# One score matmul a head over 48 stacked rows, and two normalisations moved from DVE to POOL

## The reference

```python
q = split_heads(hidden_states_query @ Wq.T + bq)      # query: the layer-normed tokens
k = split_heads(hidden_states_key @ Wk.T + bk)        # key, value: the context
v = split_heads(hidden_states_key @ Wv.T + bv)
scores = einsum('bhqd,bhkd->bhqk', q * 16 ** -0.5, k) + (1 - mask) * -10000.0
ctx = einsum('bhqk,bhkd->bhqd', softmax(scores), v)   # 16 heads
```

## Time and profile before

| | us |
|---|---|
| three runs | 1442.6, 1450.26, 1454.12 (median 1450.26) |
| the profiled execution | 1443.42, with a span of 1441.8 |
| PE busy | 1264.8 (88%) |
| DVE busy | 1092.9 (76%) |
| ACT busy | 1003.9 (70%) |
| POOL busy | 827.7 (57%) |
| first phase | from 0 to about 465, its loop from 26 on |
| mean granted clock of PE | 0.944 of full speed |

### The profile page before, as it was taken

One profiled execution on the slowest core, in us unless ns is written; L12 is line 12 of the kernel. 1 busy time (PEld: TensorE's weight loads), 2 busy tenths in 40 slices (PEclk: granted clock), 3 DMA queues, 4 the chain that ended last, 5 costly groups with the idle time before them and its releaser, 6 DMA issues. The chain is left out here.

```text
span 1441.8 us, 44028 instructions
## 1 busy us (share of the span) xinstructions
PE 1264.8 (88%) x13508; PEld 916.7 (64%) x13508; DVE 1092.9 (76%) x3110; ACT 1003.9 (70%) x2584; POOL 827.7 (57%) x1204
## 2 busy tenths in 40 slices
PE   5999999999985599999998999999999985389994
PEld 3788888888864245656665556656566653278993
DVE  4899999999984268887887877878788873367772
ACT  3988788887883368787776777777787872155662
POOL 3645444454455445777676776777677675045663
PEclk9999999999997699999999999999999996599997
DMA  6233343333400148877666766767576784753323
GB/s 172 86 120 112 106 121 98 118 99 121 120 24 17 48 92 160 159 137 148 136 148 136 151 137 140 141 145 156 122 146 138 146 186 85 285 173 60 61 35 74
DMA packets 303968, 175.19 MB, mean 122 GB/s; under 512 B 250234, under 2 KB 291586, under 8 KB 300720
## 3 DMA queue, kind: packets, MB, share of 16 engines
q1 hardware_dynamic: 287632, 130.94, 40.8%
q0 software_dynamic: 13168, 35.80, 9.8%
q10 hardware_dynamic: 3024, 6.47, 1.6%
HBM read 64.48 MB, written 41.96 MB: 74 GB/s over the span
## 5 line engine op out<-in xcount | busy, mean ns | idle before, releaser
L1663 ACT ACTIVATE b_prob<-b_prob,b_top 112x487 f32<-112x487 f32 x256 | 178.9, 699 | 42.8 <-DVE b_top L1789 40.9
L1296 POOL TENSOR_TENSOR b_halves<-b_prob,b_halves 112x487 f16<-112x487 f32 x128 | 152.3, 1190 | 88.4 <-ACT b_halves L1688 86.6
L1474 PE MATMUL b_ps_p<-w_s,b_tok_s 128*128 128x512 f16 (+1 forms) x768 | 187.7, 381 | 5.6 <-DVE b_k_s L1776 5.3
L1474 PE MATMUL b_ps_p<-b_tok_s,w_s 128*128 128x487 f16 x768 | 188.0, 384 | 4.7 <-POOL b_tok_s L1290 3.7
L1789 DVE CUSTOM_DVE_ANT_0 b_prob<-b_ps_s,b_keep 112x487 f32<-112x487 f32 x256 | 167.7, 656 | 32.1 <-PE b_ps_s L1567 31.8
L701 ACT ACTIVATE a_prob<-a_prob,a_top 112x375 f32<-112x375 f32 x256 | 156.4, 611 | 4.5 <-DVE a_top L837 3.4
L1688 ACT ACTIVATE b_halves<-b_prob 112x487 f16<-112x487 f32 x256 | 156.0, 609 | 0.4
L837 DVE CUSTOM_DVE_ANT_0 a_prob<-a_ps_s,a_keep 112x375 f32<-112x375 f32 x256 | 138.6, 541 | 21.8 <-PE a_ps_s L593 19.2
L1582 PEld LDWEIGHTS b_ps_o<-b_v_s,b_pT 128*128 128x128 f16 (+1 forms) x3072 | 124.9, 100 | 32.7 <-DMA b_pT<-b_halves 11.0
L1582 PE MATMUL b_ps_o<-b_v_s,b_pT 128*128 128x64 f16 (+1 forms) x3072 | 136.1, 195 | 9.0 <-DMA b_pT<-b_halves 8.9
L842 DVE TENSOR_TENSOR a_pT<-a_ps_t,a_pT 125x336 f16<-125x336 f32 x256 | 128.6, 503 | 18.4 <-ACT a_pT L708 12.4
(11 more groups left out here) (262 smaller groups left out, 3063.0 us busy)
## 6 DMA issues: line engine op xcount, KB each, us to landing
xs<-a_blank SPq DMA_DIRECT2D x14, 1032.0 KB, 4.0
c_w_pool<-w_split SPq DMA_DIRECT2D x8, 1600.0 KB, 10.9
b_wch_f<-in_w_experts POOLq DMA_DIRECT2D x32, 384.0 KB, 4.9
w_split<-b_wch_s POOLq DMA_DIRECT2D x32, 384.0 KB, 4.0
a_ctx_f<-in_ctxT SPq DMA_DIRECT2D x16, 375.0 KB, 3.9
a_k_stack<-a_k_s SPq DMA_DIRECT2D x64, 93.8 KB, 2.8
b_ctx_t<-in_ctx SPq DMA_DIRECT2D x16, 375.0 KB
c_xt<-xs SPq DMA_DIRECT2D x35, 129.0 KB, 2.5
```

The source lines that it names most:

```text
L1296: pool.tensor_tensor(halves[:, h % TURN, LO, 0:NK], prob[:, h % RING, 0:NK], halves[:, h % TURN, HI, 0:NK], ALU.subtract).then_inc(s_lo[1], 1)
L1474: last = pe.matmul(out, sta(a, k), mov(m, k), start=(k == 0 and n == 0), stop=(k == tiles - 1 and n == 2))
L1663: act.activation(prob[:, h % RING, 0:NK], prob[:, h % RING, 0:NK], ACT.Exp, bias=top[:, h % RING:h % RING + 1], scale=-1.0, accum_out=sums ...
```

## The change

Each head now gets 48 rows of its own: three parts of 16 rows, for the queries HI, HI, LO and for the keys HI, LO, HI, so that one matmul adds up the three products. Even heads stand in rows 0 to 47, odd heads in rows 64 to 111, in `q_stack` and `k_stack` (8 heads beside each other in the free dimension). A head's scores are one matmul of 48 rows and 375 columns. The queries are no longer doubled: PE makes them with 12 matmuls for 24, ACT moves them out with 2 instructions for 4, and POOL splits 224 columns for 448. To get into the stacked rows, keys and queries go through DRAM: one DMA writes all halves out (`keys_out`, `queries_out`), SP waits until it has landed, and six DMAs of 16 rows each read them back (`stack_keys`, `stack_queries`). SP issues `keys_out` ahead of the tokens of batch b+2, and `stack_queries` behind `clear_rows`. The zeroing of `q_masked` falls away. Wq is loaded with half its columns left out, in two DMAs of 256-byte pieces, and DVE rearranges the bias of the queries with two small copies.

`norm_x` and `norm_x1` move from DVE to POOL, each right behind its `deviation`.

```diff
-        wq_s = wqkv[:, :, :, 0:512].rearrange("p s k (g m) -> p s k g m", g=GROUPS)
-        wk_s = wqkv[:, :, :, 512:768]
-        wv_s = wqkv[:, :, :, 768:1024]
-        wg_s = wqkv[:, :, :, 1024:1024 + E]
-        bq_c = sb("bq_c", [128, GROUPS], F32)
+        wq_s = wqkv[:, :, :, 0:D]
+        wk_s = wqkv[:, :, :, D:2 * D]
+        wv_s = wqkv[:, :, :, 2 * D:3 * D]
+        wg_s = wqkv[:, :, :, 3 * D:3 * D + E]
+        bq_g = sb("bq_g", [128, GROUPS], F32)
+        bq_c = sb("bq_c", [128, KT], F32)
...
-        q_f = sb("q_f", [128, GROUPS * T], F32)
-        q_s = sb("q_s", [128, 2, GROUPS * T], F16)
-        q_masked = [sb(f"q_masked{i}", [128, 2, 4, GROUPS * T], F16) for i in range(2)]
+        q_f = sb("q_f", [128, KT, T], F32)
+        q_s = sb("q_s", [128, 2, KT, T], F16)
+
+
+        STACK = 3 * D0
+        Q_PARTS, K_PARTS = (HI, HI, LO), (HI, LO, HI)
+        q_stack = [sb(f"q_stack{i}", [128, H // 2, T], F16) for i in range(2)]
         k_s = sb("k_s", [128, 2, 2, C], F16)
-        k_stack = [sb(f"k_stack{i}", [128, GROUPS, C], F16) for i in range(2)]
+        k_stack = [sb(f"k_stack{i}", [128, H // 2, C], F16) for i in range(2)]
         v_s = [sb(f"v_s{i}", [128, NB0, H, 2, D0], F16) for i in range(2)]
...
-        QMASK = 16 * 8
+        NSTACK = 16 * 6
...
-            sp.dma_start(wqkv_f[:, :, 0:512], wq).then_inc(s_wq, 16)
-            sp.dma_start(wqkv_f[:, :, 768:1024], wv).then_inc(s_wv, 16)
-            sp.dma_start(wqkv_f[:, :, 1024:1024 + E], wg).then_inc(s_wv, 16)
+            sp.dma_start(wqkv_f[:, 0, 0:D].rearrange("p (g n) -> p g n", g=GROUPS),
+                         wq[:, 0, :].rearrange("p (g n) -> p g n", g=GROUPS)[:, :, 0:64]).then_inc(s_wq, 16)
+            sp.dma_start(wqkv_f[:, 1, 0:D].rearrange("p (g n) -> p g n", g=GROUPS),
+                         wq[:, 1, :].rearrange("p (g n) -> p g n", g=GROUPS)[:, :, 0:64]).then_inc(s_wq, 16)
+            sp.dma_start(wqkv_f[:, :, 2 * D:3 * D], wv).then_inc(s_wv, 16)
+            sp.dma_start(wqkv_f[:, :, 3 * D:3 * D + E], wg).then_inc(s_wv, 16)
...
+            def keys_out(c, par):
+
+                need_all(sp, settled, (s_ihi, 6, c, P_K + 2), (s_ifree, PI, c, P_K + 2), (s_kstack, NSTACK, c - 1, 0))
+                sp.dma_start(k_dram[par], k_s[:, :, :, :]).then_inc(s_kout, 16)
+
             def stack_keys(c, par):
 
-
-                need_all(sp, settled, (s_ihi, 6, c, P_K + 2), (s_ifree, PI, c, P_K + 2), (s_score, H, c - 1, 1))
+                need_all(sp, settled, (s_kout, 16, c, 16), (s_score, H, c - 1, 1))
+                rows = k_dram[par].rearrange("(r a d) s t c -> a s d r (t c)", a=2, d=D0)
                 for a in range(2):
-                    for part in (HI, LO):
-                        sp.dma_start(k_stack[par][64 * part:64 * part + 64, a::2, :],
-                                     k_s[64 * a:64 * a + 64, part, :, :]).then_inc(s_kstack, 16)
-
-            def mask_queries(c, par):
-
-
-                need_all(sp, settled, (s_qlo, 1, c, 1), (s_score, H, c - 1, 1))
-                for m in range(4):
-                    for row in (D0 * m, 64 + D0 * m):
-                        sp.dma_start(q_masked[par][row:row + D0, :, m, :], q_s[row:row + D0, :, :]).then_inc(s_qmask, 16)
+                    for i, part in enumerate(K_PARTS):
+                        sp.dma_start(k_stack[par][64 * a + D0 * i:64 * a + D0 * (i + 1), :, :].rearrange("d (r t) c -> d r (t c)", t=KT),
+                                     rows[a, part]).then_inc(s_kstack, 16)
+
+            def queries_out(c, par):
+
+                need_all(sp, settled, (s_qlo, 1, c, 1), (s_qstack, NSTACK, c - 1, 0))
+                sp.dma_start(q_dram[par], q_s[:, :, :, :]).then_inc(s_qout, 16)
+
+            def stack_queries(c, par):
+
+                need_all(sp, settled, (s_qout, 16, c, 16), (s_score, H, c - 1, 1))
+                rows = q_dram[par].rearrange("(r a d) s t n -> a s d r (t n)", a=2, d=D0)
+                for a in range(2):
+                    for i, part in enumerate(Q_PARTS):
+                        sp.dma_start(q_stack[par][64 * a + D0 * i:64 * a + D0 * (i + 1), :, :].rearrange("d (r t) n -> d r (t n)", t=KT),
+                                     rows[a, part]).then_inc(s_qstack, 16)
...
+                if ahead(b, 1):
+                    keys_out(b + 1, 1 - par)
                 if ahead(b, 2):
                     load_tokens(b + 2)
                 if ahead(b, 1):
                     stack_keys(b + 1, 1 - par)
-                    mask_queries(b + 1, 1 - par)
+                    queries_out(b + 1, 1 - par)
                 clear_rows(b)
+                if ahead(b, 1):
+                    stack_queries(b + 1, 1 - par)
                 if not ahead(b, 1):
                     load_residual(b)
                 if not first(b):
                     store(b - 1)
 
             load_tokens(1)
+            keys_out(0, 0)
             stack_keys(0, 0)
-            sp.wait_ge(s_zq, 2)
-            mask_queries(0, 0)
+            queries_out(0, 0)
+            stack_queries(0, 0)
...
+            def norm_x(c):
+
+                need(pool, s_rstd, 1, c, 1, settled)
+                need(pool, s_item, PI, c, 0, settled)
+                pool.tensor_scalar(xn[:, :], x_in[:, :], mv[:, 0:1], rstd[:, 0:1], ALU.subtract, ALU.mult).then_inc(s_xn, 1)
+
+            def norm_x1(c):
+
+                need(pool, s_rstd1, 1, c, 1, settled)
+                need(pool, s_ditem, DI, c, 0, settled)
+                pool.tensor_scalar(xn1[:, :], x1[:, :], mv1[:, 0:1], rstd1[:, 0:1], ALU.subtract, ALU.mult).then_inc(s_xn1, 1)
...
-                need_all(pool, settled, (s_ifree, PI, c, P_Q + 1), (s_qmask, QMASK, c, 0))
-                pool.tensor_copy(q_s[:, HI, :], q_f[:, :]).then_inc(s_qhi, 1)
+                need_all(pool, settled, (s_ifree, PI, c, P_Q + 1), (s_qout, 16, c, 0))
+                pool.tensor_copy(q_s[:, HI, :, :], q_f[:, :, :]).then_inc(s_qhi, 1)
                 need(pool, s_qhi, 1, c, 1)
-                pool.tensor_tensor(q_s[:, LO, :], q_f[:, :], q_s[:, HI, :], ALU.subtract).then_inc(s_qlo, 1)
+                pool.tensor_tensor(q_s[:, LO, :, :], q_f[:, :, :], q_s[:, HI, :, :], ALU.subtract).then_inc(s_qlo, 1)
...
                 if ahead(b, 1):
                     deviation_x(b + 1)
+                    norm_x(b + 1)
                 if not first(b):
                     residual(b - 1)
                     deviation_x1(b - 1)
+                    norm_x1(b - 1)
                 if ahead(b, 1):
                     mask_bias(b + 1, 1 - par)
                     split_queries(b + 1)
@@ -488,6 +527,7 @@
             split_context(0)
             mask_bias(0, 0)
             deviation_x(0)
+            norm_x(0)
             split_queries(0)
             split_context(1)
...
-                    for g in range(GROUPS):
-                        last = product(ps[:, g * T:(g + 1) * T], lambda a, t: wq_s[:, a, t, g, :],
+                    for j in range(KT):
+                        last = product(ps[:, j * T:(j + 1) * T], lambda a, t: wq_s[:, a, t, j * 128:(j + 1) * 128],
...
             def scores(b, par, h):
-                g, m = h // 4, h % 4
                 if h == 0:
-                    need(pe, s_qmask, QMASK, b, QMASK)
-                    need(pe, s_kstack, 64, b, 64)
+                    need(pe, s_qstack, NSTACK, b, NSTACK)
+                    need(pe, s_kstack, NSTACK, b, NSTACK)
 
                 need(pe, s_max, H, b, h - 1)
-                for part in (HI, LO):
-                    last = pe.matmul(ps_s[h % 2][0:T, 0:C], q_masked[par][:, part, m, g * T:(g + 1) * T],
-                                     k_stack[par][:, g, :], start=(part == HI), stop=(part == LO))
-                last.then_inc(s_score, 1)
+                rows = slice(64 * (h % 2), 64 * (h % 2) + STACK)
+                pair = KT * (h % 8 // 2) + h // 8
+                pe.matmul(ps_s[h % 2][0:T, 0:C], q_stack[par][rows, pair, :], k_stack[par][rows, pair, :],
+                          start=True, stop=True).then_inc(s_score, 1)
...
-                    for g in range(GROUPS):
-                        last = act.activation(q_f[:, g * T:(g + 1) * T], ps[:, g * T:(g + 1) * T], ACT.Identity, bias=bq_c[:, g:g + 1])
+                    for j in range(KT):
+                        last = act.activation(q_f[:, j, :], ps[:, j * T:(j + 1) * T], ACT.Identity, bias=bq_c[:, j:j + 1])
...
-                        need(act, s_kstack, 64, c, 0)
+                        need(act, s_kout, 16, c, 0)
...
-            act.wait_ge(s_const, 48)
+            act.wait_ge(s_const, 50)
...
-            def norm_x(c):
-
-                need(dve, s_rstd, 1, c, 1)
-                need(dve, s_item, PI, c, 0)
-                dve.tensor_scalar(xn[:, :], x_in[:, :], mv[:, 0:1], rstd[:, 0:1], ALU.subtract, ALU.mult).then_inc(s_xn, 1)
-
-            def norm_x1(c):
-
-                need(dve, s_rstd1, 1, c, 1)
-                need(dve, s_ditem, DI, c, 0)
```

(39 more changed lines are left out.)

2 lines of the change are left out of this document (1 added, 1 removed).

## The result

The changed kernel takes 1569.55 us (median of 4 runs, 1562.33 to 1586.93) against 1446.72 (4 runs, 1442.6 to 1454.12): the ratio is 1.083, 95% interval 1.074 to 1.091. The forecast was 1467 with a range up to 1480, and slower by over 1% as the likeliest sign. The sign was right, the size wrong by some 100 us.

A forecast was written before the change was run, and what follows sets the result against it. PE was taken to bound the kernel, DVE close behind. Loop +19.2, start +1.7 and end -3.9 gave +17.0 on 1450.26, so 1467 us; own range 1460 to 1478, stated range 1430 to 1480.

The forecast's parts named there:

- PE's need and the price of the switch: First-phase loop: PE needs 24.83 of 25.74 us a batch; switching to half the array adds 0.17 us a step.
- Rivals 1 and 2: First-phase scores: no switch paid, 24.0 a batch, 1424 us (chance 0.16); or half paid, 1441 us (chance 0.16).
- What the waits take up: PE's waits in a batch: later PE absorbs 0.75 us, including half the gate's 0.33; net +1.37, so 27.1 a batch.
- So it earns nothing: Normalisations to POOL: 0.4 us each there; DVE falls to 23.2 a batch, covered by PE at 27.1, so no gain.
- DMAs of a middle batch: Loop's DRAM round trip of queries: done at 252.9, before the batch's end at 257.5, so costed at nothing.
- Rival 3: Step 0 of a batch: stacked operands come late; at 1 us late 15 us more, 1482 us; chance 0.07.
- Start: Before the first scores: keys, then queries, go through DRAM, landing in 2.0 us each; +1.7 us, bounds +0.5 and +4.
- scores after 30: Sign at the kernel's start: first scores before 27 or after 30 us would make the start's term wrong.
- Last batch: Last batch's x1 normalisation, ahead of L455 on POOL: returns 1.9 us waiting and about 2.0 of slow stretch, -3.9.
- the sign named for a wrong term: Last batch: x1's normalisation on POOL lasting over 1 us would make the -3.9 wrong.
- The clock stays 1.00: Sign of a right forecast: in the changed kernel's timeline the granted clock remains 1.00, with a batch of 27.1 us.
- 14 x 1.37: First-phase loop: 14 of 16 batches each pay PE's extra 1.37 us, +19.2 us in all.

The follow-up runs named there:

- run 5: Changed kernel with both normalisations back on DVE (the change of the scores alone), DVE's code placed by 16 memsets: 1473.62 us, ratio 1.021.
- run 1: Changed kernel with DVE's code moved by 24 one-element memsets that do nothing else: 1492.51 us, ratio 1.028.
- run 6: Kernel before with only the normalisations on POOL, DVE's code placed by 24 memsets so its loops stay in the engine: 1463.11 us, ratio 1.013.
- Run 9: Whole-array 112-row score matmul, normalisations on DVE, code placed, and ACT's 2 MB expert-weight load issued only once the first queries are stacked: 1443.29 us, ratio 0.998.
- run 7: Changed kernel with one whole-array 112-row score matmul per head (zeros outside its 48 rows), normalisations on DVE, code placed: 1446.57 us, ratio 0.999.
- run 3: Kernel before with only the normalisations moved to POOL, code not placed, so five fetches a turn were expected: 1506.68 us, ratio 1.038.
- run 8: Changed kernel with 112-row score matmuls, normalisations on POOL, code moved by 124 memsets to bring the changed kernel's fetches: 1510.98 us, ratio 1.045.

## Why the prediction was wrong

**PE's need and the price of the switch: right.** 0.10 to get in, 0.10 for the transposes' weights, +0.17 a step were forecast; 0.29, 0.58 and 0.42 stand in the trace, and run 5 has PE at 26.85 a batch against 26.95. Reading it off the second phase's 64-row matmuls carried over to 48 rows, at rows 0 and 64 alike. Rivals 1 and 2 are out.

**What the waits take up: right in kind, a little short.** In run 5 no wait of PE is left, the gate's too, of which I had kept half; the scores cost 1.1 us a batch for 1.37.

**"So it earns nothing" (normalisations): the price failed.** 0.35 to 0.52 was taken from the mask bias, an instruction of POOL with immediate operands. The normalisation reads two scalars from each partition and takes 1.23 us for 256 elements, three times DVE's 0.40; that the scalars are what makes it dear is likely, but was not run apart. It stands on the way from the tokens to PE, and costs 0.7 us a batch in run 1 and 1.25 in run 6. With it a batch is 27.55 in run 1, for the forecast 27.1. The same half had a second failure, below: its two instructions left DVE's program.

**DMAs of a middle batch: right.** PE waited for no stacked operand in the loop. Rival 3 is out.

**Start: failed in one term.** +5.9 us for +1.7, beyond the bound of +4. The write of the keys to DRAM was priced by the query DMAs of the loop, of 28 KB for 375. At 13 us the 2 MB load of ACT and the next context are on the same DMA engines: 9.2 us for 2.0. Run 9 shows the load to be the cause. The text had named the sign of it: scores after 30.

**Last batch: failed.** 1.8 of the 1.9 us of waiting came back, though the normalisation took more than 1 us, the sign named for a wrong term. The 2.0 for the slow stretch did not: the clock fell earlier, with no long wait of PE ahead, and stayed at half for 20.5 us. The last two batches cost 5.9 us instead of giving back 3.9. That stretch is not a matter of 48 rows: run 7, with one matmul of 112, has 17.1 us of it from 416.5, where the kernels with two score matmuls a head have 3.4 to 10.2 at a time. In the earlier trace rows DVE's 2.34 us span both instructions of POOL, so it was kept out for the two and not for one.

**The clock stays 1.00, and 14 x 1.37: the step that failed.** The term for the loop was +19.2 us; the profiled execution has +111.7. Nothing in the sum was about code. I counted what each removed instruction takes, but not that code behind it moves. Six recorded instructions fewer ahead of DVE's loop made it need one more piece than stays. That is 80 of the 112 us of the loop, some 30 of them only together with the new scores. The earlier trace rows show nothing of instruction fetches; the DMA view of the loop before, with no instruction queue in it, had the condition by its absence. The Trainium skill, page "Advanced Engine Details and Errata", section "ISA Cache", gives each engine but TensorE a store of 32 KB for code, in lines of 16 KB. The total fits what the runs show, if four pieces of 8,192 bytes are what is kept; the line size does not.

**Without the fetches it would still have been low.** Run 1 takes 1492.5, 25 us above the 1467. Its 53.7 us of span over the kernel before are +32.1 in the 14 batches (for 19.2: POOL's normalisations and the clock of the first ones), +6.2 at the start, +3.4 in the last two batches, and +12.0 behind the first phase, which I had at nothing and which lies within what this part differs by between runs.

## What to carry to other kernels

A loop that fits the engine's code store by a few instructions is a hidden condition: before and after an edit, look for the instruction queue in the DMA view of one turn, and for a wait "from issue" behind the branch; if it appears, move the loop with a few idle instructions ahead of it before judging the edit. Test the halves of a change apart, code placed alike, since here, placed alike, the halves cost 1.3 and 2.1% and both 2.8, and the rest of the 8% comes with the placing. Price an instruction on another engine by a row with the same kinds of operands, not only the same size.

## What the runs showed of the hardware

DVE's code comes in pieces of 8,192 bytes. In the kernels run, a first loop with 192, 208, 210 or 262 recorded instructions ahead of it (295 or 305 long) stayed; with 186, 292 or 314 it was fetched, five pieces a turn. The second stop of the changed kernel puts the end of a piece at about 190 of this count. With one end every 128 from there, the loops that stayed touch three pieces and those that were fetched touch four. That fits a store of four pieces, of which one is filled ahead, so that a loop over four evicts its own start; it is a reading of seven positions, and the capacity was not measured apart.

A stop of all engines has a price beyond its length. After PE stood 3.6 to 4.6 us in the loop, the granted clock was at half for 6.8 us with two score matmuls of 128 rows (run 3), 6.8 or 10.2 with one of 112 (run 8), and 24 to 34 with one of 48 (the changed kernel, where the longest stretch follows the shortest stop). Why it stays down longest with 48 rows is open, and the normalisations on DVE were not run with such stops. At the start, the same scores behind stops of 13.9 and 14.8 us had the clock back 4 us after the first of them (run 5) and 36 us after it (run 1).
